# First FFN group of a fused attention and ternary FFN kernel: one chunk's statistics, three weight sums and a transpose moved by one unit, and one wait on a bank removed

## The reference, cut to what matters

```python
def _quantize(w):
    gamma = jnp.mean(jnp.abs(w))
    return jnp.clip(jnp.round(w / (gamma + EPS)), -1.0, 1.0)
...
S = bt[:, :, None] * S + dt[:, :, None] * kv
ot = jnp.einsum('bk,bkv->bv', qt, S)
...
x1 = _bitlinear(x, w1)
x2 = _bitlinear(x, w2)
hidden = jax.nn.sigmoid(x1) * x2
return _bitlinear(hidden, w3)
...
x = x + _L0_attn_ref(_layernorm(x, axis=-1), ...)
x = x + _L0_ffn_ref(_layernorm(x, axis=-1), L0_ffn_w1, L0_ffn_w2, L0_ffn_w3)
```

## Time and profile before

| | us |
|---|---|
| median of 3 runs | 318.64 (318.29 to 318.87) |
| the profiled execution: time | 318.46 |
| the profiled execution: span of its instructions | 316.7 |
| PE busy | 306.8 of 316.7 |
| DVE, ACT, POOL busy | 235.2, 183.2, 177.2 |

### The profile page before, as it was taken

One profiled execution on the slowest core, in us unless ns is written; L12 is line 12 of the kernel. 1 busy time (PEld: TensorE's weight loads), 2 busy tenths in 40 slices (PEclk: granted clock), 3 DMA queues, 4 the chain that ended last, 5 costly groups with the idle time before them and its releaser, 6 DMA issues.

```text
span 316.7 us, 7197 instructions
## 1 busy us (share of the span) xinstructions
PE 306.8 (97%) x2548; PEld 213.2 (67%) x2548; DVE 235.2 (74%) x524; ACT 183.2 (58%) x413; POOL 177.2 (56%) x419
## 2 busy tenths in 40 slices
PE   7999999999999989999999999999999999999996
PEld 5888779874544434467888744778976448888545
DVE  6879989899989898897767879669677823455401
ACT  3587986969863673624666554346655406777200
POOL 7298325589993655997334896734467302444300
PEclk9999999999999999999999999999999999999999
DMA  6999900575862156630000039200000790000011
GB/s 180 380 387 395 398 24 0 67 135 100 129 108 50 34 85 133 103 99 17 3 3 0 3 64 211 91 2 2 3 2 0 90 245 33 3 0 2 2 66 66
DMA packets 55027, 29.43 MB, mean 93 GB/s; under 512 B 46800, under 2 KB 47568, under 8 KB 54992
## 3 DMA queue, kind: packets, MB, share of 16 engines
q1 hardware_dynamic: 54672, 28.97, 36.4%
q10 hardware_dynamic: 320, 0.00, 0.1%
HBM read 13.89 MB, written 4.19 MB: 57 GB/s over the span
## 4 chain that ended last, share of the span: by engine, by line
PE 64%; DVE 11%; ACT 6%; DMA 5%; issue 5%; POOL 4%; SPq 3%; DVEq 0%; POOLq 0%; ACTq 0%
PE ffn L1638 23%; PE ffn L1620 9%; PE pd L1638 8%; PE pd L1620 8%; PE ffn L1436 5%; DVE X L1125 3%; PE lev L1512 3%; DMA x_sb<-in_L_attn_x_dram 3%; PE pd L1446 2%; ACT q L793 2%; DMA w12T<-q 2%; SPq L404 2%; DVE sc L1187 2%; PE lev L1469 1%; ACT w12T L781 1%
## 5 line engine op out<-in xcount | busy, mean ns | idle before, releaser
L1638 PE MATMUL ffn<-w_nat,w12T 128*128 128x256 f16 x468 | 63.1, 273 | 0.0
L646 POOL TENSOR_TENSOR xnT<-xnT,q 128x256 f32<-128x256 f32 x33 | 24.3, 736 | 65.5 <-ACT xnT L975 45.0
L1638 PEld LDWEIGHTS ffn<-w_nat,w12T 128*128 128x128 f16 x468 | 45.1, 98 | 8.5 <-issue 1.5
L1620 PE MATMUL ffn<-w3T,w_nat 128*128 128x512 f16 x220 | 48.3, 379 | 0.0
L1591 PE MATMUL ffn<-w_nat,w12T 128*128 128x512 f16 x176 | 39.2, 379 | 2.3 <-DVE xnT L1330 2.3
L1620 PEld LDWEIGHTS ffn<-w3T,w_nat 128*128 128x128 f16 x220 | 21.6, 98 | 25.8 <-issue 0.6
L1638 PE MATMUL ffn<-w_nat 128*128 128x256 f16 x216 | 32.4, 273 | 0.0
L1591 PEld LDWEIGHTS ffn<-w_nat,w12T 128*128 128x128 f16 x176 | 16.9, 98 | 22.7 <-issue 3.8
L1436 PE MATMUL ffn<-xnT,w_proj 128*128 128x256 f32 x128 | 29.5, 384 | 1.2 <-ACT xnT L722 0.8
L1381 DVE TENSOR_TENSOR w_nat<-xnT,w_nat 128x512 f16<-128x512 f32 x33 | 23.1, 699 | 9.1 <-ACT w_nat L983 8.5
L1365 DVE SCALAR_TENSOR_TENSOR q<-ffn,w_nat 128x256 f32<-128x256 f32 x33 | 14.0, 424 | 21.0 <-PE ffn L1638 20.9
(11 more groups left out here) (194 smaller groups left out, 642.1 us busy)
## 6 DMA issues: line engine op xcount, KB each, us to landing
x_sb<-in_L_attn_x_dram SPq DMA_DIRECT2D x16, 256.0 KB, 8.3
out_dram<-x_sb SPq DMA_DIRECT2D x15, 256.0 KB, 2.1
w_nat<-in_L_ffn_w_dram SPq DMA_DIRECT2D x2, 1536.0 KB, 12.1
w_nat<-in_L_ffn_w_dram SPq DMA_DIRECT2D x2, 1408.0 KB, 15.5
w_nat<-in_L_ffn_w_dram SPq DMA_DIRECT2D x2, 1280.0 KB, 12.9
w_proj<-in_L_attn_Wv_dram SPq DMA_DIRECT2D x1, 256.0 KB, 5.5
wo<-in_L_attn_Wo_dram SPq DMA_DIRECT2D x1, 256.0 KB, 13.4
out_dram<-x_sb SPq DMA_DIRECT2D x2, 128.0 KB, 1.7
```

The lines of the kernel that those rows point to most:

```text
L646: nc.gpsimd.tensor_tensor(hid32[:, u % 2, HP:2 * HP], sig[:, u % 2, HP:2 * HP], up[:, u % 2, HP:2 * HP], ALU.mult).then_inc(pool_hid, 1)
L1620: done = nc.tensor.matmul(down_bank(g, m)[:, :], hid_at(g, part, j, m), w3T[:, j, :], start=n == 0, stop=n == 2 * HT - 1)
L1638: done = nc.tensor.matmul(out[:, 0:HP], weights[:, t, u * P:(u + 1) * P], tokens[:, part, t, :], start=first and t == 0 and part == 0, sto ...
```

## The change

In the lists that hold during group 0, chunk 2's statistics (norm2) and its apply come one unit later on DVE (5 to 6, 6 to 7), its xlo too (8 to 9), its xhiN and xhiS on ACT (7 to 8, 8 to 9) and its turn on SP (9 to 10). The weight sum n = 2 moves from unit 5 to 6, n = 4 from 7 to 8. POOL's list is not touched. product1(1, 1) no longer waits for the add_outs of group 0; product1 of the later groups waits as before.

```diff
-        DVE_NEXT_FAST = {k: v for k, v in DVE_AFTER.items() if k != "xlo"}
-        DVE_NEXT_FAST |= {"sums": (None, 12), "xlo": (8, 12), "xloS": (None, 12)}
-        ACT_NEXT_FAST = {"gt": (2, 7), "oT": (4, 9), "xhiN": (7, 12), "xhiS": (8, 12)}
+        DVE_NEXT_FAST = {"chain0": (0, 5), "chain1": (0, 5), "masks": (2, 7), "state": (4, 9), "resid": (5, 11),
+                         "norm2": (6, 11), "apply": (7, 12), "sums": (None, 12), "xlo": (9, 12), "xloS": (None, 12)}
+        ACT_NEXT_FAST = {"gt": (2, 7), "oT": (4, 9), "xhiN": (8, 12), "xhiS": (9, 12)}
         POOL_NEXT_FAST = {"fetch": (0, 3), "norm2": (6, 11), "sums0": (7, None), "sums1": (7, None), "xlo": (7, None)}
-        SP_NEXT_FAST = {"turn": (9, 12)}
+        SP_NEXT_FAST = {"turn": (10, 12)}
...
-        T_AT = {4: (3,), 5: (2,), 7: (4,), HT + 2: (1,)}
+        T_AT = {4: (3,), 6: (2,), 8: (4,), HT + 2: (1,)}
...
                 else:
-                    pe.wait_ge(y_ready, g * DT - 2 if u == 0 else g * DT)
+                    if u == 0:
+                        pe.wait_ge(y_ready, g * DT - 2)
+                    elif g > FAST[0]:
+                        pe.wait_ge(y_ready, g * DT)
                     pe.wait_ge(steps_done, 2)
```

## The result

| | us | ratio to before |
|---|---|---|
| before, 10 executions | 318.73 (318.29 to 319.06) | 1 |
| changed, 10 executions | 319.56 (318.98 to 320.44) | 1.0026 (95%: 1.0015 to 1.0037) |

The change costs 0.83 us (319.56 - 318.73). The profiled execution of the changed kernel took 320.12 us with a span of 318.4; its mean granted clock of TensorE was 0.995, where before it was 1.000. Of the ten executions five had 0.995 (319.49 to 320.30, median 320.06) and five 1.000 (318.98 to 320.44, median 319.12). That split carries about half of the loss.

What follows compares the result with a forecast made beforehand. PE is busy 306.8 of 316.7 us, but from 119 to 145 DVE and POOL set the pace. Profiled 318.46 plus 0.6 for late resid, with PE's gains and the wait at 0, gives 319.1 us; range 317.4 to 320.1.

Steps and rivals of the forecast that it cites:

- the likeliest case: Whole kernel: resid of chunk 3 0.6 us later, PE's gains 0, 319.1 us; chance 0.45.
- Part 1: Unit 5 on DVE: norm2 of chunk 2 and weight sum 2 leave, so PE's 1.41 us wait before unit 8 goes.
- Part 2: DVE from 99.77: 9.49 us of queued work, so apply of chunk 2 ends at 109.3, 3.2 us later.
- Part 3: Behind apply: weight sum 4 holds POOL's sums, 5.2 us not 3.48; through ACT, resid of chunk 3 comes 0.6 us later.
- Part 4: Other moves: PE's 2.3 us won go back into waits for w3 in down m = 0 and for add_outs at the seam.
- Part 5: product1(1, 1) on PE: starts up to 0.4 us earlier, but "o" of chunk 4 waits for DVE's mask; worth 0.
- Rival 1: POOL's sums not held by weight sum 4, ending at 112.9; resid 1.1 us earlier, 317.4 us; chance 0.15.
- rivals 2 and 3: POOL: L637 ahead of unit 9's rest, about 318.6, chance 0.2; weight sum 4 ahead of L632, 319.3 to 320.1, chance 0.2.
- rival 2: L637 ahead of unit 9's rest, or resid's lateness lost in DVE idle time: no change, about 318.6; chance 0.2.

Runs made afterwards that it cites:

- second and third experiment: Second: changed kernel with weight sum 4 at unit 9, not 8, 319.44 us; third: changed kernel with xhiS at unit 10 of ACT's list, not 9, 317.77 us.
- fourth experiment: Changed kernel with seven unused extra matmuls on PE in front of the wait for block 10 of w3 in down m = 0: 319.13 us, ratio 1.0011.
- first experiment: Kernel before with only the wait of product1(1, 1) given up: 318.73 us, ratio 0.9998.
- sixth experiment: Kernel before with xhiS of chunk 2 at unit 10 of ACT's list in place of 8, nothing of the change: 318.88 us, ratio 1.0006.

## Why the prediction was right, and where it fell short

The time lay inside the range, and the likeliest case was the right mechanism with one term missing. That its 319.1 agrees with the executions at full clock (median 319.12) is in part luck: the sum starts from a profiled execution of 318.46, 0.27 below the median before, and its +0.6 came out as 0.4 or less.

- *Part 1* held: unit 8 follows the levels without a wait.
- *Part 2* held: 9.49 us from the end of unit 5 to the end of apply were predicted; from 100.17, where the product of unit 6 starts now, to 109.63 it took 9.46.
- *Part 3* held: sums of 5.2 us predicted, 109.71 to 114.96 measured; resid 0.6 us later predicted, 119.91 - 98.97 = 20.94 against 20.52 measured, so 0.4. A part of the difference is that the product of unit 6 starts 1.20 us after resid of chunk 2, not 1.32 as bn_stats did. The second and third experiment show the two links, the sums held by weight sum 4 and the work behind xhiS. L636's 2.00 us beside the weight sum, and 0.73 without it, agree with the rule of the Trainium skill that stands in the prediction ("SBUF — State Buffer", section "Who interferes with whom").
- *Part 4* failed in one sentence: that PE's waits for w3 and at the seam only give back what PE had won. The wait for w3 came out inside its bounds (0.8 to 2.4 predicted, 1.89 measured), and at the seam PE did not wait at all. But the sum counted the matmuls behind the wait at 0.218 us and had no term for the clock, and in the profiled execution they ran at half clock and took 1.7 us more; five of the ten executions have its mean clock. Down m = 0 then ended at about 126.0, on the prediction's scale of time 125.5, not at 122.1 to 123.7; DVE stood idle for 2.03 us until add_out could start, and the chain went over to PE, which the prediction had with room to spare. The fourth experiment takes just that away: 0.4 us of the median, 0.9 between the two kinds of execution (320.06 - 319.12).
- *Part 5* held: 0 for the wait, by the first experiment, on the kernel before. No run puts the wait back into the changed kernel by itself; in its profile the last add_out ends at 142.51, before product1(1, 1) starts at 143.15, so the wait would not have held PE there either.

Rival 1 was decided against by L636; rivals 2 and 3 needed other orders at the shared access, and the trace has the one of the forecast, also in its race of 0.1 us (L637 behind the rest of unit 9). The second half of rival 2, that lateness is lost again behind resid, held in part: at full clock 0.4 us there left 0.1 to 0.4 at the end.

## What to carry to other kernels

Before a step is moved later in a hand-written order, list what stands behind it on every engine that waits for it in order; here the four late sums did no harm once the sign3 and the sigmoid no longer queued behind them. A wait on the matrix engine that seems free because another engine sets the pace should be priced twice, once by its length and once with the matmuls behind it at half clock, for the executions in which the clock falls. When a change moves nearly nothing, look for the one queue that eats its gain: one more entry moved here turned 0.8 us of loss into 1.0 us of gain.

## What the runs showed of the hardware that was not expected

- A standstill of PE of 1.89 us right behind one of 0.27 was followed by more than 3 us at a granted clock of 0.5 in the profiled execution, and five of ten executions had a mean clock of 0.995. With one of 2.15 us four of six had 0.994 or 0.995; with 1.25 us it was four of twelve, with 1.05 and 1.20 in one kernel, about 8 us apart, none of eleven, and in the sixth experiment, with 1.39 before unit 8, one of twelve (320.04 us at 0.995). The kernel before has 1.41 at that place, and none of its 52 executions beside the experiments was under 0.999, so the length alone doesn't order these cases. What decides between executions of one kernel, these runs don't show.
- Two engines that want the same access took turns: POOL's L632 had waited when the rest of unit 7 ended, and it went ahead of the weight sum that was next on DVE, which then took 2.15 us in place of 1.61.
- The last transpose of w3 landed 3.5 us after its issue in the changed kernel (117.98 to 121.45), where the median of the eleven is 2.5 and the longest 4.2.
